# Other product and diagonal states in a state-space scan, and a step's side work one slot earlier

## The reference, cut to what matters

```python
xz = x @ W_in.T
xc, z = split(xz)                       # 256 channels each
xc = silu(causal_conv4(xc) + conv_b)
dBC = xc @ W_x.T                        # 64 for dt, 16 for B, 16 for C
delta = softplus(dBC[..., :64] @ W_dt.T + b_dt)
deltaA = exp(delta[..., None] * A)      # A = -exp(A_log), 16 states
BX = delta[..., None] * B[:, :, None, :] * xc[..., None]
h_t = deltaA_t * h_{t-1} + BX_t         # associative_scan over the rows
y = einsum('bldn,bln->bld', h, C) + Dp * xc
out = (y * silu(z)) @ W_out.T
```

## Time and profile before

| | |
|---|---|
| time, median of 3 runs | 1546.77 us (1543.91 to 1547.09) |
| the profiled execution | 1556.4 us, span 1554.6 us |
| mean granted TensorE clock | 0.92 |
| PE, DVE, ACT, POOL busy over the whole span | 84%, 76%, 69%, 68% |
| the scans, L694 | 512 of 1260 ns, 614.3 us busy |
| the state-space part | to about 907 us of the span |

### The profile page before, as it was taken

How to read it: one execution, slowest core, us unless ns; L and a number is a source line. 1 busy time by engine, 2 the same in 40 slices (tenths; PEclk the granted TensorE clock), 3 DMA queues, 4 the chain that set the end, 5 groups by cost and what they waited for, 6 DMA issues and landing times. The chain is left out here.

```text
span 1554.6 us, 31674 instructions
## 1 busy us (share of the span) xinstructions
PE 1309.2 (84%) x8851; PEld 1062.0 (68%) x8852; DVE 1182.9 (76%) x2467; ACT 1068.3 (69%) x2078; POOL 1060.4 (68%) x875
## 2 busy tenths in 40 slices
PE   4799999899999989998998847999989950989882
PEld 2587778778777877877787743666666640988782
DVE  2598899989898998989899943687767753476664
ACT  3888988988898798889879804676656630544441
POOL 5498788878888887888888841245444563267666
PEclk9899999999999999999999976999999965999996
DMA  2232333333233233323223314011111122222220
GB/s 63 83 96 77 97 100 90 92 100 96 78 101 96 88 95 96 91 80 102 90 84 94 105 52 123 27 35 52 50 54 54 48 65 72 59 61 74 65 61 21
DMA packets 100579, 119.16 MB, mean 77 GB/s; under 512 B 10752, under 2 KB 61634, under 8 KB 100478
## 3 DMA queue, kind: packets, MB, share of 16 engines
q1 hardware_dynamic: 94670, 104.20, 22.9%
q0 software_dynamic: 5808, 13.81, 2.5%
HBM read 99.45 MB, written 19.04 MB: 76 GB/s over the span
## 5 line engine op out<-in xcount | busy, mean ns | idle before, releaser
L821 POOL TENSOR_TENSOR cm<-hbuf,crep 128x1024 f32<-128x1024 f32 x256 | 604.9, 2370 | 134.6 <-DVE hbuf L694 134.4
L694 DVE TENSOR_TENSOR_SCAN hbuf<-abuf,hstate,bank 128x512 f32<-128x512 f32 x512 | 614.3, 1260 | 56.3 <-PE bank L375 42.9
L576 ACT ACTIVATE abuf<-delta,aneg 128x512 f32<-128x512 f32 x512 | 337.3, 712 | 71.8 <-DVE hbuf L694 71.7
L396 PE MATMUL bank<-ident,cm 128*128 128x128 f32 x2048 | 256.0, 273 | 2.6 <-POOL cm L821 2.6
L396 PEld LDWEIGHTS bank<-ident,cm 128*128 128x128 f32 x2048 | 230.4, 141 | 3.3 <-POOL cm L821 3.3
L587 ACT ACTIVATE ub<-uT,bT 128x256 f32<-128x256 f32 x512 | 217.0, 496 | 0.2
L375 PEld LDWEIGHTS bank<-bdiag,uT 128*128 128x128 f32 x1024 | 141.3, 212 | 33.2 <-issue 18.8
L378 PE MATMUL bank<-ident,ub 128*128 128x128 f32 x1024 | 141.1, 278 | 18.8 <-ACT ub L587 13.6
L375 PE MATMUL bank<-bdiag,uT 128*128 128x128 f32 x1024 | 146.4, 300 | 8.0 <-DVE hbuf L694 7.9
L378 PEld LDWEIGHTS bank<-ident,ub 128*128 128x128 f32 x1024 | 117.1, 143 | 47.1 <-DVE hbuf L694 20.4
L1530 POOL TENSOR_TENSOR b_rstd<-b_vare,half_neg 128x4 f32<-128x4 f32 x32 | 32.7, 1022 | 159.2 <-DVE b_nmean L1317 159.2
(11 more groups left out here) (204 smaller groups left out, 2538.8 us busy)
## 6 DMA issues: line engine op xcount, KB each, us to landing
crep<-c_rows SPq DMA_DIRECT2D x256, 256.0 KB, 3.2
rows<-routed SPq DMA_DIRECT2D x72, 128.5 KB
xin<-in_x SPq DMA_DIRECT2D x16, 256.0 KB, 3.7
xres<-in_x SPq DMA_DIRECT2D x16, 256.0 KB, 3.6
x_rows<-x1t SPq DMA_DIRECT2D x64, 64.0 KB
xg<-x_rows SPq DMA_DIRECT2D x16, 256.0 KB, 3.0
pk<-x_rows SPq DMA_DIRECT2D x16, 256.0 KB, 2.8
w<-in_w SPq DMA_DIRECT2D x1, 2048.0 KB, 10.1
```

The lines of the kernel that those rows point to most:

```text
L396: mm = pe.matmul(ps_y[j // 2][:, (j % 2 * CH + c) * P:(j % 2 * CH + c + 1) * P], cm[:, n % CM_RING, c, j * P:(j + 1) * P], ident[:, :], is ...
L576: e = act.activation(abuf[:, n % RING, c, :], delta[:, parity(g), c, :], ACT.Exp, scale=aneg[:, c, n:n + 1])
L694: dve.tensor_tensor_scan(hbuf[:, n % RING, c, :], abuf[:, n % RING, c, :], ps_bx[n % 2 * CH + c][:, :], hstate[:, bass.ds(g * (NST * CH) + ...
L821: pool.tensor_tensor(cm[:, n % CM_RING, :, :], hbuf[:, n % RING, :, :], c, ALU.mult).then_inc(s_cm, 1)
```

## The change

Product states are 0, 10, 12 and 14 and diagonal ones 2, 4, 6 and 8; the odd ones stay. The two diagonal buffers are taken in turn, and the semaphore counts follow. TensorE's `turn_x` goes from slot 3 to slot 2 and the second `f_dt` from 6 to 5; ScalarE's `f_xnT` from slot 5 to 4, `f_bT` from 6 to 5, softplus from 8 to 7. GpSimd makes the diagonal for state 6 in slot 3, for 8 in slot 5, and those for 2 and 4 of the next step both in slot 12; at the start it makes two instead of one.

```diff
-        PE_MADE = CH * (NST - NST // 4)
+        SPREAD, DIAG = (0, 10, 12, 14), (2, 4, 6, 8)
+        NSPR, NDIAG = len(SPREAD), len(DIAG)
+        PE_MADE = CH * (NST - NSPR)
...
+        def diag_buf(g, n):
+            return (parity(g) * NDIAG + DIAG.index(n)) % 2
...
@@ tensor: state_in and step
-                if n % 4 == 0:
+                if n in SPREAD:
...
-                if n % 4 == 2:
-                    pe.wait_ge(s_diag, g * (NST // 4) + n // 4 + 1)
+                if n in DIAG:
+                    pe.wait_ge(s_diag, g * NDIAG + DIAG.index(n) + 1)
...
-                    if n == 3 and has(g + 2):
+                    if n == 2 and has(g + 2):
                         turn_x(g + 2)
...
-                    if n == 6 and has(g + 1):
+                    if n == 5 and has(g + 1):
                         f_dt(g + 1, 1)
@@ scalar: step
-                    if n == 5 and has(g + 2):
+                    if n == 4 and has(g + 2):
                         f_xnT(g + 2)
                     if n == 5 and past(g, 1):
                         t_copy(g - 1)
-                    if n == 6 and has(g + 1):
+                    if n == 5 and has(g + 1):
                         f_bT(g + 1)
-                    if n == 8 and has(g + 1):
+                    if n == 7 and has(g + 1):
                         f_softplus(g + 1)
@@ gpsimd: step
-                    if n % 4 == 2 and n < NST - 4:
-                        diagonal(g, n + 4)
-                    elif n % 4 == 2 and has(g + 1):
-                        diagonal(g + 1, 2)
+                    if n - 1 in DIAG[:NDIAG - 2]:
+                        diagonal(g, DIAG[DIAG.index(n - 1) + 2])
+                    if n == 12 and has(g + 1):
+                        diagonal(g + 1, DIAG[0])
+                        diagonal(g + 1, DIAG[1])
...
-            diagonal(0, 2)
+            diagonal(0, DIAG[0])
+            diagonal(0, DIAG[1])
             f_u(0)
```

More of the change, by code:

```diff
@@ L181, in has @@
             return not isinstance(g, int) or 0 <= g < STEPS
-        PE_MADE = CH * (NST - NST // 4)
+        SPREAD, DIAG = (0, 10, 12, 14), (2, 4, 6, 8)
+        NSPR, NDIAG = len(SPREAD), len(DIAG)
+        PE_MADE = CH * (NST - NSPR)
         def made(g, n):
             g, n = (g - 1, n + NST) if n < 0 else (g, n)
-            return PE_MADE * g + CH * (n - (n + 3) // 4)
+            return PE_MADE * g + CH * sum(i not in SPREAD for i in range(n))
+        def diag_buf(g, n):
+            return (parity(g) * NDIAG + DIAG.index(n)) % 2
         SUMS = ((), (), (), (), (), (), (0,), (1, 2), (3, 4), (5,), (6, 7), (8,), (9,), (10,), (11,), (12,))
@@ L373, in state_in @@
                         dst = ps_bx[n % 2 * CH + c][:, j * P:(j + 1) * P]
-                        if n % 4 == 2:
-                            mm = pe.matmul(dst, uT[:, parity(g), j, c * P:(c + 1) * P], bdiag[:, n // 4 % 2, j, :],
+                        if n in DIAG:
+                            mm = pe.matmul(dst, uT[:, parity(g), j, c * P:(c + 1) * P], bdiag[:, diag_buf(g, n), j, :],
                                            start=True, stop=True)
@@ L541, in f_bT @@
                 if past(f, 2):
-                    act.wait_ge(s_diag, (f - 1) * (NST // 4))
+                    act.wait_ge(s_diag, (f - 1) * NDIAG)
                     act.wait_ge(s_ub, (f - 1) * (NST // 2))
-                    act.wait_ge(s_brep, (f - 1) * (NST // 4))
+                    act.wait_ge(s_brep, (f - 1) * NSPR)
                 act.activation(bT[:, parity(f), :, :],
@@ L689, in scan @@
                 for c in range(CH):
-                    if n % 4 == 0:
-                        dve.wait_ge(s_bu, g * (NST // 4 * CH) + n // 4 * CH + 2)
+                    if n in SPREAD:
+                        dve.wait_ge(s_bu, CH * (g * NSPR + SPREAD.index(n)) + 2)
                     else:
@@ L701, in input_product @@
                     dve.wait_ge(s_u, g + 1)
-                dve.wait_ge(s_brep, g * (NST // 4) + n // 4 + 1)
-                if past(g, 1) or n >= 4:
+                dve.wait_ge(s_brep, g * NSPR + SPREAD.index(n) + 1)
+                if past(g, 1) or n >= 2:
                     dve.wait_ge(s_scan, 2 * (g * NST + n - 2) + 2)
                 dve.tensor_tensor(ps_bx[1][:, :], u[:, parity(g), 1, :], ps_bx[0][:, :], ALU.mult).then_inc(s_bu, 1)
-                dve.wait_ge(s_bu, g * (NST // 4 * CH) + n // 4 * CH + 1)
+                dve.wait_ge(s_bu, CH * (g * NSPR + SPREAD.index(n)) + 1)
                 dve.tensor_tensor(ps_bx[0][:, :], u[:, parity(g), 0, :], ps_bx[0][:, :], ALU.mult).then_inc(s_bu, 1)
@@ L797, in f_u @@
                 if past(f, 2):
-                    pool.wait_ge(s_bu, (f - 1) * (NST // 4 * CH))
+                    pool.wait_ge(s_bu, (f - 1) * NSPR * CH)
                     pool.wait_ge(s_ut_mm, f - 1)
@@ L802, in diagonal @@
             def diagonal(g, n):
-                if n == 2:
+                i = DIAG.index(n)
+                if i == 0:
                     pool.wait_ge(s_bt, g + 1)
                     pool.sem_inc(carrier, 1)
-                if past(g, 1) or n >= 8:
-                    pool.wait_ge(s_bx, made(g, n - 8) + CH)
+                if past(g, 1) or i >= 2:
+                    pool.wait_ge(s_bx, made(g, DIAG[i - 2] - (NST if i < 2 else 0)) + CH)
                     pool.sem_inc(carrier, 1)
-                pool.affine_select(out=bdiag[:, n // 4 % 2, :, :],
+                pool.affine_select(out=bdiag[:, diag_buf(g, n), :, :],
                                    in_=bT[:, parity(g), :, n:n + 1].broadcast_to([P, TT, P]),
```

## The result

The changed kernel takes 1560.27 us (median of 13 runs, 1554.33 to 1565.79) against 1547.09 for the one before, timed beside it: 1.0086 times as long, 95% interval 1.006 to 1.0112. I had forecast 1533, some 1% faster. It is slower, and outside my range. The profiled execution has a span of 1563.3 us against 1554.6.

A forecast was written before the change was run, and what follows sets the result against it. It took TensorE's stall before B's turn, with ScalarE's chain right behind, to bound the state-space steps. Fourteen steps give -15.8 us, the start -0.6, the end +2.9: -13.5, so 1546.77 becomes 1533 us; range 1522 to 1547.

The forecast's parts named there:

- the sum of a full step: State-space step: 25.98 us from `f_delta` to decay 2, 6.4 to Z, 20.8 to `f_delta`, 0.1 for GpSimd: 53.3.
- the rival of the clock: In slots 8 to 15 short TensorE waits drop its clock, +30 us, giving 1563 us; chance 0.13.
- The stall: TensorE idles some 3.1 us before B's turn, then state 6 runs slow (3.25 against 1.95); the change removes both.
- the 0.85 us by which the mean lay above my sum: Before: mean step 54.09 us against a summed 53.24, since in most steps the stall outlasts ScalarE.
- Z to `f_delta`, 20.8: From ScalarE's table load ending its gate work (Z) to `f_delta`: 22.03 us less 1.23 for softplus moved ahead.
- `f_delta` to Z, 32.4: From `f_delta` to ScalarE's table load (Z): grows from 31.2 to 32.4 us, a loss of 1.2.
- Softplus makes `f_delta` wait 3 us: In every step VectorE's `f_delta` would wait 3 us for ScalarE's softplus, a sign expected in the profile.
- The new wait of the second dt matmul, up to 0.7 us: TensorE's `f_dt(g+1,1)` in slot 5 waits for `f_bT` between nothing and 0.7 us, covered by VectorE's lead.
- GpSimd's two diagonals: Both in slot 12, forecast 0.1 us; rival: `t_rstd` late by 0.6 to 1.25 us, 1541 to 1549, chance 0.12.
- First `f_delta`: Start of the state-space part: 1.23 us earlier by softplus, 0.6 later by the second diagonal, -0.6 in all.
- Behind the last one: After the fifteenth `f_delta`: 7 products instead of 5, 1.31 to 1.55 us each, +2.9 us.
- the signs by which I said I would be wrong: `f_delta` doesn't wait, Z over 33 us after it, `t_add` waits for `trstd`, or clock at 0.5 in slots 9 to 15.

The follow-up runs named there:

- e6: Changed kernel, same instructions and order, VectorE's loop cut so that its jump stands in slot 8 ahead of `f_delta`: 1538.18 us, 0.9918 of before.
- e3: Kernel before with the five moves by a slot alone, product and diagonal states as before: 1486.35 us, 0.9842 of before.
- e4: Changed kernel with the moves by a slot undone, leaving the new states alone: 1547.32 us, 1.0211 of before.
- e9: Changed kernel with product states 0, 8, 10, 12 and diagonal ones 2, 4, 6, 14: 1502.61 us, 0.9932 of before.
- e1: Kernel before with one wait more, VectorE's scan of state 14 waiting for its scan of state 13: 1531.44 us, 1.0107 of before.
- e11: Kernel before with VectorE's scan of state 13 waiting for its own scan of state 12: 1516.01 us, one run.
- e5: Changed kernel itself, timed again on another chip: 1563.16 us, 1.0071 of before.
- e8: Kernel before with the moves by a slot alone, timed again: 1518.73 us, 0.9783 of before.
- e7: Kernel before with the moves by a slot alone and all 16 steps written out: 1511.92 us, 0.9752 of before.

## Why the prediction was wrong

The step that failed is the sum of a full step, "25.98 + 6.4 + 20.8 + 0.1 = 53.3", taken for all fourteen: it has no term for the loop's jump. At the four jumps the runs showed 3.9 to 4.7 us of idle time on VectorE instead, which made the step 5.5 to 6.65 us longer, 23.6 us in all. Without that the sum would have held: e6, in which this wait is hidden, is 0.9918 of before, and 1533 would have been 0.991. The measured 1560 lies near the 1563 that I gave for the rival of the clock; that is chance, since e6 has the same short waits in the second half and not the time. The terms that are in the sum hold:

- *The stall.* Gone, and by the moves alone (e3 against e4). But that it "costs twice" I had read from one step and took for all. Before, the clock fell behind ten of the thirteen stalls; behind those at 285, 555 and 719 us, of 2.7 to 3.2 us, it stayed at 1.00. The first of these lies in the very step that I had added up, and the three steps with them are those of 53.24, 53.23 and 53.24 us in which softplus ended the wait. So the 0.85 us by which the mean lay above my sum goes with the falls. The row of the stall, and of state 6 behind it:

```profile
285.28 0.63 PE L332 MATMUL bank<-ident,dbc 128*128 128x128 f32 x4 [3.15 <-ACT xnT L499]
...
286.60 1.95 PE L375 MATMUL bank<-bdiag,uT 128*128 128x128 f32 x16
```

- *Z to `f_delta`, 20.8.* Measured 285.71 - 264.90 = 20.81.
- *`f_delta` to Z, 32.4.* Measured 32.67, from the row of ScalarE below. This is the loss by the new states; with the old ones it is 31.2 (e3).
- *Softplus makes `f_delta` wait 3 us.* 3.01.
- *The new wait of the second dt matmul, up to 0.7 us.* 0.63, and it costs nothing.
- *GpSimd's two diagonals.* `t_add` follows the scan of state 12 without a pause; the rival is out.
- *TensorE's clock in the second half.* The waits of 0.4 to 1.2 us that I feared are there (0.84 ahead of state 14, at most 1.0), with the clock at 1.00. So the rival did not come true in this kernel, and here the trace does not bear out what I drew from the Trainium skill ("TensorE: Matmul & The Clock Gate", section "A second HAM failure mode: psum-queue depth-cycling"). As a mechanism it is not out: in e9 the clock fell behind waits of 1.16 and 0.6 to 0.7 us. In the changed kernel it falls at the four jumps alone, behind 2.9 to 3.6 us without work.
- *First `f_delta`.* 75.46 instead of my 78.2. *Behind the last one* the gate of the last step came 77.67 us later, against 75.35 before: +2.3, forecast +2.9.

```profile
264.90 1.28 ACT L616 ACT_TABLE_LOAD   x1
```

```profile
303.44 0.65 PE L366 MATMUL bank<-ident,bT 128*128 128x128 f32 x4 [0.84 <-DVE hbuf L700]
...
338.67 1.12 PE L346 MATMUL bank<-dbc,w_dt 65*128 65x512 f32 x2 [0.63 <-ACT bT L551]
```

In the fourteen steps: 757.22 before, 741.4 forecast, 766.38 measured; 742.8 without what the jumps hold. The jumps took the gain and more. Of the signs by which I said I would be wrong one came, and only in the four long steps: the distance to Z was over 33, 39.3 in the first.

I had named no rival for it, and could have. That the ten middle steps are a loop over pairs, and that product 14 comes right ahead of the last scan of its body, is plain from the program. And the trace of the kernel before has the wait at that scan four times, 1.4 to 1.5 us, with a releaser that couldn't be right, since the scan of state 15 had had its decay long before (the decay started at 308.89, the scan at 319.54).

What stays open: how long the jump takes in itself, whether it is the issue of the instructions ahead of it that covers it (e1 shows that a wait for VectorE's own result brings the cost out, not how), and why, covered, it costs 1.2 to 1.6 us in most of these kernels and nothing in e11. No run here separates the time of the jump from the issue of the instructions behind it. Nor was it tried whether the jumps of the other engines cost anything; the 25 us that moving VectorE's alone gave leave little room for them.

## What to carry to other kernels

Where an engine's program is a loop, look for the idle time ahead of the first instruction of its body, whatever the profile names as its releaser, and put it in the sum. Keep an instruction that waits for its own engine's last result away from the end of the body, or cut the loop where the engine waits anyway: that alone gave 25 us here, with no instruction changed. And of an edit with several parts measure each alone: here one half gave 2%, and the other took it away and 1% more.

## What the runs showed of the hardware

- A jump on VectorE costs 3.8 to 5.0 us of idle time if the scan ahead of it waits for VectorE's own last result (the changed kernel, e1, e4, e5), and 0 to 1.6 us if it doesn't (before, e3, e8, e9, e11).
- Such a gap reaches TensorE as 1.9 to 3.6 us without work, and its granted clock then fell to 0.50 at fifteen of the sixteen jumps of the changed kernel, e1, e4 and e5; at one, behind 2.87 us, it stayed at 1.00, and the step was 1.7 us shorter.
- The length of one pause doesn't decide whether the clock falls: in the kernel before it stayed at 1.00 behind three pauses of 2.7 to 3.2 us, and in e9 it fell behind 1.16 and 0.6 to 0.7 us. In the changed kernel pauses of up to 1.0 us, and in e3 and e7 of up to 1.25 us, left it at 1.00 in every full step.
- The same kernel took 1547, 1514, 1551 and 1513 us (medians) on the four occasions, 2.5% apart (the two of 1514 and 1513 on one chip), which is more than most of the effects here.
